# Swapping two TensorE steps in a 32-head attention loop: the projection of group n + 2 ahead of the maxima of group n + 1

## The reference, cut to what matters

```python
qkv = x @ w_qkv                        # 128 -> 3 * 32 * 32
s = (q @ k.T) * 32 ** -0.5             # 256 x 256 for each head
p = softmax(s, axis=-1)
out = concat_heads(p @ v) @ w_out + b_out
```

## Time and profile before

| | us |
|---|---|
| median of 3 runs (1319.93 to 1321.64) | 1320.36 |
| the profiled execution | 1321.37 |
| its span | 1319.7 |
| PE busy, share of the span | 1170.9, 89% |
| DVE busy | 911.6, 69% |
| ACT busy | 689.6, 52% |
| POOL busy | 234.0, 18% |

### The profile page before, as it was taken

One profiled execution on the slowest core, in us unless ns is written; L12 is line 12 of the kernel. 1 busy time (PEld: TensorE's weight loads), 2 busy tenths in 40 slices (PEclk: granted clock), 3 DMA queues, 4 the chain that ended last, 5 costly groups with the idle time before them and its releaser, 6 DMA issues. The chain is left out here.

```text
span 1319.7 us, 27471 instructions
## 1 busy us (share of the span) xinstructions
PE 1170.9 (89%) x10598; PEld 790.7 (60%) x10598; DVE 911.6 (69%) x2410; ACT 689.6 (52%) x1307; POOL 234.0 (18%) x337
## 2 busy tenths in 40 slices
PE   7769999999999999998997899889778898799885
PEld 4446767776777676775554666545555465556542
DVE  5463383375499968798976698866788766756466
ACT  2234454555554565445565546657427555377524
POOL 3320121112110130012201013010120112301122
PEclk8889999999999999999998999989999999899987
DMA  7001111211112100210000010000000000000000
GB/s 287 16 1 48 49 34 32 65 41 41 33 49 78 35 17 25 72 33 17 1 1 2 2 34 9 1 1 2 2 1 1 2 1 2 1 2 2 1 1 33
DMA packets 23288, 35.59 MB, mean 27 GB/s; under 512 B 4584, under 2 KB 12920, under 8 KB 22904
## 3 DMA queue, kind: packets, MB, share of 16 engines
q1 hardware_dynamic: 23160, 33.83, 8.1%
HBM read 32.77 MB, written 1.05 MB: 26 GB/s over the span
## 5 line engine op out<-in xcount | busy, mean ns | idle before, releaser
L2238 DVE TENSOR_REDUCE arena<-banks 128x4 f32<-128x1024 f32 x128 | 150.6, 1218 | 74.6 <-PE banks L2066 73.9
L1354 PEld LDWEIGHTS banks<-WE,arena 128*128 128x128 f32 x1536 | 180.0, 192 | 24.5 <-issue 22.6
L1354 PE MATMUL banks<-WE,arena 128*128 128x128 f32 x1536 | 182.7, 276 | 0.1
L1398 ACT ACTIVATE arena<-banks,BC 128x512 f32<-128x512 f32 x192 | 129.5, 691 | 99.9 <-PE banks L1338 99.6
L1338 PE MATMUL banks<-XT,WE 128*128 128x512 f32 x384 | 179.7, 604 | 0.0
L2218 ACT ACTIVATE arena<-banks 128x1024 f32<-128x1024 f32 x128 | 124.1, 1022 | 71.2 <-PE banks L2090 71.2
L1438 DVE SCALAR_TENSOR_TENSOR R<-banks,arena,R 128x128 f32<-128x128 f32 x256 | 72.0, 344 | 107.0 <-PE banks L1354 106.4
L613 ACT COPY arena<-banks 128x512 f32<-128x512 f32 x100 | 57.7, 589 | 120.4 <-PE banks L608 36.7
L2319 POOL TENSOR_TENSOR arena<-arena 128x256 f32<-128x256 f32 x56 | 43.6, 778 | 381.6 <-ACT arena L2200 381.6
L1338 PEld LDWEIGHTS banks<-XT,WE 128*128 128x128 f32 x384 | 69.6, 193 | 66.7 <-issue 65.7
L1900 DVE TENSOR_TENSOR arena<-arena 128x512 f32<-128x512 f32 x144 | 100.5, 698 | 3.9
(11 more groups left out here) (329 smaller groups left out, 2121.3 us busy)
## 6 DMA issues: line engine op xcount, KB each, us to landing
WE<-in_weights SPq DMA_DIRECT2D x64, 256.0 KB, 2.9
WE<-in_weights SPq DMA_DIRECT2D x64, 128.0 KB, 2.2
WS<-in_weights SPq DMA_DIRECT2D x1, 2368.0 KB, 14.3
RW<-in_rows SPq DMA_DIRECT2D x1, 1032.0 KB
XALL<-in_x SPq DMA_DIRECT2D x4, 256.0 KB, 10.9
out_dram<-arena SPq DMA_DIRECT2D x4, 256.0 KB, 2.3
WS<-in_weights SPq DMA_DIRECT2D x1, 900.0 KB, 9.0
WS<-in_weights SPq DMA_DIRECT2D x1, 645.0 KB, 9.1
```

Of the source, the lines that this page charges most:

```text
L1354: ins = PE.matmul(v[:, tile(t)], self.HT[:, e % 2, j, tile(t)], self.W[:, (8 * i + e) % RING, 1, j], start=j == 0, stop=j == self.J - 1)
L1398: A.activation(self.HT[:, e % 2, j], psum.view(f"{self.L}.h{i}.{e}.{j}"), ACT.Relu, bias=bcol(self.p + "_b1", e * self.J + j))\
L2238: V.tensor_reduce(big.mx[:, 2 * pair:2 * pair + 2], v, AX.X, ALU.max, negate=True).then_inc(dve.read(f"big.m{i}.{n}.{pair}"), 1)
```

## The change

In the loop of `big_pe` two calls change places. Nothing is added or removed, and the slots of the other engines stay as they are.

```diff
             for n in range(GROUPS + 1):
+                if n + 2 < GROUPS:
+                    project(n + 2)
                 if n + 1 < GROUPS:
                     maxima(n + 1)
-                if n + 2 < GROUPS:
-                    project(n + 2)
                 if n < GROUPS:
                     scores(n)
                 if n >= 1:
```

## The result

The changed kernel takes 1334.12 us (median of 4 runs, 1333.85 to 1336.89) against 1321.0 us before (4 runs, one more than stood ahead of the prediction): ratio 1.0101, 95% interval 1.008 to 1.0122, so 13.1 us slower. The prediction was 1334, in a range of 1319 to 1348. The profiled execution took 1333.85 us, its span 1332.1 against 1319.7.

The account below looks back on a forecast made before the run. PE, busy 89% of the span, was taken as the bound, its order deciding. The terms 17.6 + 6.9 + 0.5 - 4.6 - 6.7 gave +13.7 us, on the median 1334, in a range of 1319 to 1348.

Parts of the forecast that it names:

- (a): 22 passes bound by PE: scores wait for ACT's copy of v, 0.8 us more per pass, +17.6 us.
- (b): Passes with e.1 on v and m.0: scores wait for a reduction beginning 1.51 later, +6.9; two first passes +0.5.
- (c): 21 passes where DVE is late: 1.22 us won each, partly lost as reductions move later; -4.6 us together.
- (e): Five late passes with waits of 3.0 to 3.4 us no longer lose clock: 5 x -1.3 = -6.7 us.
- (d): Six passes among 11 to 13: the projection's wait for ACT's hold gives way to the copy-of-v wait; 0 us.
- bound of 2.6 us: PE waits in late passes, split into some 0.7 and 2.1, stay under 2.6 us and so keep the full clock.
- ten or fewer: Sign in PE's waits: the scores' waits (L2085) for DVE's reduction (L2238) fall from 21 to ten or fewer.
- no pass with 4.4 us from L2085 to L2076: Sign: no pass takes 4.4 us from the scores' load to the next L2076.
- The tie to DVE is what matters: Rival: the 21 late reductions don't move and each gives 1.22 us; -7 us, about 1313, chance 0.09.
- no-change rival: Late-pass and clock gains meet the losses of the other passes: 1318 to 1323 us, chance 0.07.
- clock rival: The 0.7 us idle lowers the clock in 27 passes, 1.3 more each: +35 us, about 1376, chance 0.04.

Follow-up runs that it names:

- e8: Kernel before with the projection first in all passes except the six with the longest waits for DVE; 1356.08 us, ratio 1.0245.
- e7: Kernel before, order and banks kept, with 12 filler matmuls while PE waits in five passes whose scores wait over 3 us for DVE; 1315.8 us, ratio 0.9954.
- e9: Kernel before with the projection first in ten passes only: the six with the longest waits for DVE and four more; 1306.57 us, ratio 0.9884.
- e1: Kernel before with the projection ahead of the maxima but the banks taken in the old order; 1397.3 us, ratio 1.0575.
- e4: Kernel before with the projection first only in the six passes whose scores wait longest for DVE; 1311.41 us, ratio 0.9929.
- e10: Second set of runs of the six-pass kernel (kernel before, swapped only in the six longest-waiting passes), on the ten-pass kernel's chip; 1308.54 us, ratio 0.989.
- e6: Kernel before with two more ACT copies of 256 columns ahead of the q, k and v copies in each group; 1321.69 us, ratio 0.9998.

## Why the prediction was right, step by step

The 56 passes of the profiled execution after, against their lengths before, in the groups of the prediction:

| group | passes | predicted us | measured us |
|---|---|---|---|
| (a) bound by PE, e.1 on qk and v | 22 | +17.6 | +19.5 |
| (b) e.1 on v and m.0, and the two first passes | 7 | +7.4 | +4.9 |
| (c) and (e) DVE late, with the clock | 21 | -11.3 | -14.2 |
| (d) hold | 6 | 0 | 0.0 |
| all | 56 | +13.7 | +10.2 |

**(a)** was right in its mechanism and, for 21 of its 22 passes, in its size: 0.75 each. Two errors inside the pass cancelled. I put the projection's load at 0.22 behind L2076, though the earlier trace rows show 0.07 (739.69 to 739.76), so everything behind it came some 0.14 early, the copy's end at 2.64 and not 2.78; and PE was released 0.11 or 0.23 behind it in place of 0.10. Pass 9 of chunk 1 alone gave 3.7, a case I had not seen:

```profile
908.42 1.65 ACT L563 ACTIVATE XALL<-R,shift,rstd 128x128 f32<-128x128 f32 x4
...
910.92 0.39 ACT L2179 COPY arena<-banks 128x256 f32<-128x256 f32 x1
...
911.56 0.61 PE L2085 MATMUL banks<-arena,ones 32*128 32x512 bf16 x4 [2.28 <-ACT arena L2179]
...
911.94 1.94 PE L2090 MATMUL banks<-arena 32*128 32x256 f32 x16
```

Another chunk's normalisation stands ahead of the copies on ACT. Before, that delay was free, since nobody waited for the copies; now it reaches the scores, and the granted clock of the pass is 0.81. With the same delay in e8, a wait of 2.17, the clock stayed at 1.00 and the pass took 7.21 in place of 8.89: of the 3.7, some 1.6 is the clock.

**(b)** was too high by 2.5 us: passes 0 and 1 of chunk 2 became shorter by 0.7 and 0.1, where I had a part of the +0.5 and +1.2. The 0.7 is not the swap's: pass 0 of chunk 2 ran at a clock of 0.74 before and at 1.00 after, and it takes the same 5.90 us in e7 and e9, which do not swap it. Three passes came at +1.4, near my 1.5.

**(c)** held in its parts: D to L2076 is 3.2 instead of 4.4, and the reduction begins 0.4 to 0.6 later in four of the six longest passes. With (e) it was too small for pass 2 of chunk 1 (13.64 to 9.92, where the two terms give 2.5); e7 shows that the clock alone is 2.8 there, not 1.3.

**(e)** was too hopeful in its rule and near in its sum by luck. Four of the five passes kept the full clock (pass 7 above: 1.00), and by e7 these four are worth 7.4 us, more than the 6.7 that I had for five. Pass 5 of chunk 2 did not, though its wait was cut into 0.91 and 1.82:

```profile
1027.84 0.40 PE L2085 MATMUL banks<-arena,ones 32*128 32x512 bf16 x4 [0.91 <-ACT arena L2179]
...
1030.92 1.94 PE L2103 MATMUL banks<-arena,group_column 128*32 128x256 f32 x16 [1.82 <-DVE arena L2238]
```

With pass 9 of chunk 1 the changed kernel has two such passes where the one before had these five and pass 0 of chunk 2. The bound of 2.6 us that I took from the earlier trace rows is refuted on both sides by the last section. The rule of the Trainium skill that I set against it (TensorE: Matmul & The Clock Gate, "A second HAM failure mode: psum-queue depth-cycling") does not show in the passes that it was meant for: eight in a row, idle for 15%, ran at a granted clock of 1.00.

**The sum.** The passes give 10.2 us of the profiled execution's 12.5, and 1.8 of the rest lies ahead of the first changed instruction. It is no effect of the change: the first L2076 of chunk 0's loop stands at 660.0 to 663.9 us in the profiles of before, after, e1 to e4 and e7 to e10, whose programs are alike up to there. So that 1334 was hit this closely is luck; the steps' own error is some 3.5 us, and inside it an ACT delay missed (+1.9) stands against first passes overrated (-2.5) and late passes underrated (-2.9).

**The signs.** Two of those named did not come: eleven waits of L2085 for L2238 are left, not ten or fewer, and "no pass with 4.4 us from L2085 to L2076" was no sign at all, since that stretch now holds the values' wait: pass 5 of chunk 0 has 4.44 at a clock of 1.00.

**The rivals.** "The tie to DVE is what matters" was half right and worth knowing: it holds in six passes (e4) and not in the other fifty together (e8). The point named, that late passes follow passes whose reduction the swap pushes back, accounts for little of it: in the changed kernel the six still win 12.3 us, against 15.8 when they alone are swapped, and 2.2 of the difference is pass 5 of chunk 2 with its lowered clock. The rival lost most in the other fifteen late passes, which win 2.0 us together and not 1.22 each; nine of them, by (c), were late by less than the maxima move. The no-change rival and the clock rival fell with the result.

## What to carry to other kernels

With a ring of banks, moving an instruction also moves every later product to another bank, and so changes who waits for whom; follow the takes before moving anything, and price both halves. A step that costs where its engine is the bound can pay where another engine is late: choose it pass by pass from the waits of the trace, here 10 to 14 us instead of a loss of 13. And when a wait moves to another engine, look at what else that engine runs ahead of the awaited instruction in the same slot: what was free delay there has become a stall.

## What the runs showed of the hardware

Whether a wait lowers the clock did not follow from the wait's length. 2.43 us before the matmul at 1003.01 left it at full speed; 2.28 before that at 911.56 and the pair of 0.91 and 1.82 did not, and 0.91 with 1.71 (pass 7 of chunk 0) did. Nor did it follow for the same wait in the same pass: pass 7 of chunk 0 had 3.30 and a clock of 0.83 before, and in e6, with order and banks as before, 3.31 and 1.00:

```profile
714.98 0.40 PE L2086 MATMUL banks<-arena,ones 32*128 32x512 bf16 x4 [3.31 <-DVE arena L2243]
...
718.04 0.11 PEld L2077 LDWEIGHTS banks<-ident,shift_parts 128*128 128x128 bf16 x2 [0.41 <-issue]
```

From there to L2077 it is 3.06 us, where it was 4.39. In pass 13 of chunk 1 a wait of 2.00 left the clock at 1.00 before and lowered it to 0.83 in e4. So what one profile says of the clock in a pass need not hold for the next execution: the passes that (e) counts had the low clock in the profile before, but in e6 two of the five (5 and 7 of chunk 0) ran at 1.00 without any filler. What decides it stays open, and the clock's price rests on e7's five executions (1311.2 to 1316.7 us, against 1320.1 to 1326.2 for the kernel before) and not on its trace alone.

A low clock cost 1.3 to 1.7 us in most of these passes, 2.8 in pass 2 of chunk 1 and 0.7 in pass 0 of chunk 2, and twelve filler matmuls in the wait bought it back. PE's release behind an ACT copy took 0.11 or 0.23 us, which makes the difference between passes of 5.84 and 5.95 us.
